# A GNN kernel on one core: a GpSimd drain behind each indirect transfer of the scatter and of the edge stage

## The chip, the cores and the metric

The kernel runs on one core of a Trainium2 chip. The metric is the time of one execution on the device, in microseconds (us). The names of the engines in the profile are PE (TensorE, matrix products; PEld is its weight load), DVE (VectorE), ACT (ScalarE), POOL (GpSimd) and SP (SyncE, which here issues DMAs). A name with a q behind it (POOLq) is the sequencer of that engine, which issues its instructions and waits on its semaphores.

## The reference

Four graph layers run one behind the other over a graph of 6,250 nodes with 128 features and 106,250 edges (two directions of 50,000 random edges, and a loop at each node), sorted by `dst`. Behind each stands a residual addition and a layer norm.

```python
edge_index = jnp.stack([src, dst])
x = _layernorm(x + _L0_gnn_ref(...), axis=-1)   # m = h @ weight[i]; agg = segment_sum(m[src], dst); h = gru_cell(agg, h)   (3 times)
x = _layernorm(x + _L1_gnn_ref(...), axis=-1)   # hypergraph: segment sums of h[row] by col, of e_feat[col] by row, batch norm, relu
x = _layernorm(x + _L2_gnn_ref(...), axis=-1)   # attention: softmax over src of leaky_relu(s1[src] + s2[dst]), sum of mapped[dst]
# L3:
e_in = jnp.concatenate([x[src], x[dst]], axis=-1)
edge_new = relu(e_in @ We1 + be1) @ We2 + be2
agg = jax.ops.segment_sum(edge_new, dst, num_segments=x.shape[0])
x = _layernorm(x + (x + mlp(concatenate([x, agg]))), axis=-1)
```

## The kernel before, in words

**The matrix.** The layers 0 to 2 don't work on the list of edges but on a dense matrix of edge counts, `adj_t` (and its transpose `adj_s`), 16-bit floats in DRAM. It is stored in 13 groups of rows; each group is read in 13 turns of 512 KB. It is first filled with zeros by DMA. Then the counts are put in: VectorE works out, from the sorted edges, for each of 832 columns of 128 edges a cell number and a value (`cell_at`, `cell_val`), and GpSimd writes each column with one indirect transfer, 128 cells of two bytes (`scatter_cells`, L1394 to L1396).

**The order of the scatter** stands in the loop at L1411 to L1437, written out by hand. The 832 columns are cut into ten units: six slabs of 104 columns and four pieces. Before a slab GpSimd waits until VectorE has its cells (`cells_ready`), before the first ones also until the zeros are there (`zeroed`). In the middle of a unit it waits with `unit_written` (L1407 to L1409) until the transfers of the unit before have landed, and counts `slab_done` up. Ahead of the fifth slab (`n == SL // 2`) stand 8 small transfers (L1427) and 7 gathers of pairs of edges (L1431), with waits for VectorE (`ext_moved`, `pairs_ready`); the first stage of the other engines ends with what these bring. Behind the last unit but one stand three transfers for cells beyond the columns (`scatter_ext`, L1400), and behind the last unit, which is waited for, three more gathers (L1444).

**The first pass** over the matrix (L493 to L650) starts when that first stage has ended. SP loads a tile of `adj_t` per turn (L498), ScalarE casts it for the matrix products of layer 0, PE multiplies it (L567, L568) and turns it over (transposes, L575), VectorE moves what is turned out of PSUM (L623), and ScalarE stores it as `adj_s`. There are 181 turns: 12 groups of 13, then 12 turns for the rows behind them, and the last group (number 11 of 0 to 12) with 13. SP holds each group back until the scatter has passed the units that touch it:

```python
            def group_there(g):
                sp.wait_ge(S("slab_done"), sp.value_load(need[0:1, g:g + 1], min_val=1, max_val=len(UNITS)))
```

and the last group until all of them are written. After the first pass come the remaining passes of the layers 0 to 2, in which GpSimd has no work.

**The edge stage** (layer 3) does work on edges, 110 chunks of 8 tiles of 128 edges. For every tile GpSimd gathers 128 rows of 512 bytes from a table of the nodes (`edge_pool`, L887), 880 gathers in all, into a ring of four chunks (`row_ring`, `HOT` = 4). It waits ahead of each chunk for `idx_ready`, the chunk's indices that ScalarE copies into a ring of four (`indices`, L905). ScalarE does that for chunk c + 4 at the end of its own turn of chunk c, when the rows of chunk c have landed and VectorE has added them. For each tile PE multiplies one-hot matrices with the part of `dst` (L942); VectorE adds the gathered rows to it (L965 to L980), ScalarE applies the relu (L927), PE sums the edges of a block (L953) and VectorE adds the sums to `acc` (L990). All five engines go over the chunks with `edge_turns` (L869 to L877), and semaphores link them.

Of the kernel before, what the change touches and what calls it, by code (L numbers as in the profile page):

```python
# [123 lines left out]
def wait(eng, sem, value):  # L124

    if isinstance(value, int) and value <= 0:
        return
    if isinstance(sem, Count):
        eng.wait_ge(sem.sem, value + sem.base)
    else:  # L130
        eng.wait_ge(sem, value)  # L131
# [10 lines left out]
def gnn(nc, d):  # L142
    ctx = ExitStack()
    with ctx:
# [199 lines left out]
        def S(name):  # L344
            if name not in made:
                made[name] = sem(name)
            return made[name]
# [521 lines left out]
        def edge_turns(eng, body):  # L869

            for c in range(PEELED):
                body(c, c % HOT, 0, c)
            with eng.Fori(0, EDGE_LOOPS) as i:
                for h in range(HOT):
                    c = PEELED + h
                    body(HOT * i + c, c % HOT, i + c // HOT, None)
            for c in range(PEELED + HOT * EDGE_LOOPS, CHUNKS):  # L877
                body(c, c % HOT, c // HOT, c)

        def edge_pool(pool):  # L880
            idx_ready = S("idx_ready")

            def body(c, slot, use, at):
                wait(pool, idx_ready, c + 1)
                pool.sem_inc(rows_opened, 1)
                for u in range(CH):
                    nc.gpsimd.indirect_dma_start(  # L887
                        row_ring[slot][:, u, :], None, table[0:N, :],
                        bass.IndirectOffsetOnAxis(idx_ring[:, slot * CH + u:slot * CH + u + 1], 0),
                    ).then_inc(half_landed[2 * slot + u // 4], 16)  # L890
            edge_turns(pool, body)

        def edge_sp(sp):
# [422 lines left out]
        def _(pool):  # L1316
# [77 lines left out]
            def scatter_cells(out, cells, name, c):  # L1394
                nc.gpsimd.indirect_dma_start(out, bass.IndirectOffsetOnAxis(cells[:, c:c + 1], 0), cell_val[:, c:c + 1],  # L1395
                                             None).then_inc(S(name), 16)  # L1396

            def scatter_ext(out, j, name):
                for k in range(EXT_BLOCKS):
                    nc.gpsimd.indirect_dma_start(out, bass.IndirectOffsetOnAxis(ext_i[:, j + k:j + k + 1], 0),  # L1400
                                                 ext_val[:, k:k + 1], None).then_inc(S(name), 16)

            def zeroed(at):
                pool.wait_ge(S("zeroed"), pool.value_load(need[P - 1:P, at:at + 1], min_val=1, max_val=len(ZEROED)))
                pool.sem_inc(rows_opened, 1)

            def unit_written(n):  # L1407
                pool.wait_ge(S(f"at_written{n % 2}"), 16 * sum(UNITS[n % 2:n + 1:2]))
                pool.sem_inc(S("slab_done"), 1)  # L1409

            def unit_from(n):  # L1411
                return n * SLW if n < KEPT else KEPT * SLW + sum(PIECES[0:SCATTER_ORDER[n - KEPT]])

            for n in range(len(UNITS)):
                if n < KEPT:
                    pool.wait_ge(S("cells_ready"), n + 1)
                else:
                    pool.wait_ge(S("relaid"), 16 * (5 + 2 * len(PIECES)))
                if n < 2:
                    zeroed(GROUPS + n)  # L1420
                if n == 2:
                    pool.wait_ge(S("zeroed"), len(ZEROED))
                if n == SL // 2:
                    pool.wait_ge(S("cells_ready"), SL + 1)
                    pool.wait_ge(S("ext_moved"), 48)
                    for t in range(SL):
                        nc.gpsimd.indirect_dma_start(ext_node, bass.IndirectOffsetOnAxis(ext_i[:, 24 + t:25 + t], 0),  # L1427
                                                     ext_i[:, 24 + SL + t:25 + SL + t], None).then_inc(S("ext_stored"), 16)
                    pool.wait_ge(S("pairs_ready"), 1)
                    for g in range(TG):  # L1430
                        nc.gpsimd.indirect_dma_start(pair_rows[:, g, :], None, edges.rearrange("(t e) a -> t (e a)", e=P),  # L1431
                                                     bass.IndirectOffsetOnAxis(pair_idx[:, g:g + 1], 0)
                                                     ).then_inc(S("pairs_in"), 16)
                for c in range(UNITS[n]):
                    if n and c == min(SC, UNITS[n] // 2):
                        unit_written(n - 1)
                    scatter_cells(adj_t, cell_at, f"at_written{n % 2}", unit_from(n) + c)  # L1437
                if n == len(UNITS) - 2:
                    pool.wait_ge(S("cells_ready"), SL + 2)
                    scatter_ext(adj_t, 16, "at_ext")  # L1440
            unit_written(len(UNITS) - 1)

            for k in range(EXT_BLOCKS):
                nc.gpsimd.indirect_dma_start(ext_w[:, k:k + 1], None, hyper_row[0:N, :],  # L1444
                                             bass.IndirectOffsetOnAxis(ext_i[:, k:k + 1], 0)).then_inc(S("ext_stored"), 16)
            edge_pool(pool)


# [1194 lines left out]
```

## Time and profile before

| | before |
|---|---|
| median of 3 runs | 6,140.44 us |
| lowest, highest run | 6,117.9 and 6,144.16 us |
| profiled execution | 6,150.24 us |
| its span in the trace | 6,148.5 us |
| its mean granted clock of TensorE | 0.79 of full speed |

The profile is taken from one execution. Its span runs from the first to the last instruction, 1.7 us less than that execution's own time. A page sums it up: busy time by engine, the costliest groups of instructions (source line, engine, operation, what is written from what, the count, the busy time in us and the mean duration in ns, and then the idle time of the engine ahead of them with what ended it). "Issue" as such a cause is time in which the engine waited for no other engine that the profile shows. Stretches can be cut out of the trace, with each engine's busy time and number of instructions (x) in them.

### The profile page before, as it was taken

What the parts mean: (1) busy time and instruction counts of PE and PEld (TensorE: products, weight loads), DVE (VectorE), ACT (ScalarE), POOL (GpSimd) and SP (SyncE); (2) the same over time, 40 slices, a digit from 0 to 9 for tenths busy, and PEclk for the clock granted to TensorE, in tenths of its full rate; (3) what the DMA queues carried; (4) which work ended last, traced back from release to release, by engine and by line L of the source; (5) the groups of instructions that cost most, each with busy time, mean ns of one, the idle gap of its engine ahead of it and who ended that gap; (6) DMA issues with size and microseconds to landing.
All of it is one profiled execution on the core that took longest, in us unless ns stands there. A gap on an engine that the chain in (4) does not pass through costs nothing. (4 is left out here: it accounts for less than half of the span.)

```text
span 6148.5 us, 81008 instructions
## 1 busy us (share of the span) xinstructions
PE 4033.3 (66%) x23848; PEld 3300.6 (54%) x23849; DVE 3243.5 (53%) x7745; ACT 2296.2 (37%) x3162; POOL 1771.6 (29%) x1769
## 2 busy tenths in 40 slices
PE   5432482111599889899699897899973444444446
PEld 3211251000477677787588685899973443344335
DVE  6321375000499888787766446688862333333334
ACT  0000011000366555555455554788852222222223
POOL 4677303777200000000000000000025555655562
PEclk7655696555799999999899897999986666666667
DMA  9600000000599468388188782244432222222221
GB/s 363 248 1 0 0 3 27 14 14 21 191 368 368 161 231 283 111 287 283 56 290 285 210 286 82 90 149 148 145 107 74 76 78 73 81 79 74 74 81 49
DMA packets 316927, 854.94 MB, mean 139 GB/s; under 512 B 84546, under 2 KB 108800, under 8 KB 316666
## 3 DMA queue, kind: packets, MB, share of 16 engines
q1 hardware_dynamic: 204092, 616.07, 29.7%
q10 hardware_dynamic: 57120, 177.22, 7.7%
q0 software_dynamic: 55456, 58.46, 3.8%
q8 instruction: 130, 2.13, 0.1%
q14 instruction: 129, 1.06, 0.0%
HBM read 666.57 MB, written 185.01 MB: 139 GB/s over the span
## 5 line engine op out<-in xcount | busy, mean ns | idle before, releaser
L887 POOL DMA_INDIRECT big<-table,idx_ring x880 | 875.2, 995 | 3592.9 <-ACT idx_ring L905 3331.9
L1395 POOL DMA_INDIRECT adj_t<-cell_val,cell_at x832 | 861.1, 1035 | 366.5 <-issue 352.2
L744 PE MATMUL ps<-tiles_r,stage_r 128*128 128x512 f32 x2028 | 807.4, 398 | 33.4 <-ACT tiles_r L702 27.6
L623 DVE TENSOR_SCALAR_CACHE_REDUCE big<-ps 128x512 f16<-128x512 f16 (+2 forms) x724 | 430.1, 652 | 602.3 <-remote 493.8
L990 DVE TENSOR_TENSOR acc<-ps,acc 128x128 f32 x880 | 255.4, 290 | 734.0 <-remote 484.9
L927 ACT ACTIVATE stage<-stage 128x512 f32<-128x512 f32 x220 | 135.7, 630 | 1102.3 <-DVE stage L980 915.2
L1757 PE MATMUL ps<-big,ident_h 128*128 128x104 bf16 (+1 forms) x2880 | 364.6, 265 | 272.7 <-issue 270.8
L953 PE MATMUL ps<-big,stage 128*128 x1760 | 330.1, 356 | 280.1 <-issue 132.4
L751 PE MATMUL ps<-stage,big 128*128 128x130 f32 x4046 | 464.0, 277 | 17.6 <-DVE big L839 15.4
L751 PEld LDWEIGHTS ps<-stage,big 128*128 128x128 f32 x4046 | 459.7, 193 | 18.3 <-issue 14.5
L953 PEld LDWEIGHTS ps<-big,stage 128*128 128x128 f32 x1760 | 297.9, 259 | 307.0 <-issue 306.8
L702 ACT CAST tiles_r<-onehot 128x1024 fp32r<-128x1024 f16 x338 | 354.8, 1050 | 288.1 <-PE ps L746 144.8
L744 PEld LDWEIGHTS ps<-tiles_r,stage_r 128*128 128x128 f32 x2028 | 387.1, 191 | 128.3 <-issue 25.5
L1757 PEld LDWEIGHTS ps<-big,ident_h 128*128 128x128 bf16 x2880 | 234.3, 107 | 404.7 <-issue 341.1
L2152 DVE TENSOR_TENSOR big<-stage 128x1248 bf16<-128x1248 f32 x192 | 272.2, 1455 | 329.6 <-remote 231.4
L746 PE MATMUL ps<-tiles_r,lower_r 128*128 128x512 f32 x1016 | 402.1, 396 | 0.0
L676 ACT ACTIVATE big<-big,cols,stage 128x512 f32 (+1 forms) x508 | 371.5, 802 | 80.5 <-PE ps L751 68.9
L746 PE MATMUL ps<-tiles_r,lower_late 128*128 128x512 f32 x1012 | 400.9, 396 | 0.0
L942 PE MATMUL ps<-rows,stage 128*128 128x128 f32 x864 | 173.0, 333 | 290.2 <-issue 286.5
L942 PE MATMUL ps<-onehot,stage 128*128 128x128 f32 x896 | 182.5, 333 | 258.4 <-issue 244.2
L523 ACT CAST tiles_r<-onehot 128x2048 fp32r<-128x2048 f16 (+2 forms) x91 | 162.6, 1789 | 451.7 <-DVE big L623 269.1
L942 PEld LDWEIGHTS ps<-rows,stage 128*128 128x128 f32 x864 | 150.8, 244 | 316.3 <-issue 312.4
(427 smaller groups left out, 7908.6 us busy)
## 6 DMA issues: line engine op xcount, KB each, us to landing
onehot<-adj_t SPq DMA_DIRECT2D x332, 512.0 KB
big<-adj_t SPq DMA_DIRECT2D x332, 512.0 KB
onehot<-adj_s SPq DMA_DIRECT2D x170, 512.0 KB
adj_t<-rows ACTq DMA_DIRECT2D x13, 6656.0 KB
adj_s<-big ACTq DMA_DIRECT2D x157, 512.0 KB
stage<-local_rows SPq DMA_DIRECT2D x110, 512.0 KB
big<-adj_s SPq DMA_DIRECT2D x84, 512.0 KB
x_fm<-adj_s SPq DMA_DIRECT2D x84, 512.0 KB
```

Of the source, the lines that this page charges most:

```text
L623: last = nc.vector.tensor_scalar(turned[turn % RING][:, j, of, :].rearrange("p m c -> p (m c)"), flips[turn % 2][:, j, of, :].rearrange("p ...
L676: nc.scalar.activation(tile32[s][:, m * GW:(m + 1) * GW], r_rows[:, bass.ds(g * GW, GW)], ACT.Relu, bias=col(MINUS_ONE), scale=stage_nm[:, ...
L702: nc.scalar.copy(tile_r[s][:, 0:TW // 2], raw_tile(p, s)[:, 0:TW // 2]).then_inc(S("cast_act"), 1)
L744: nc.tensor.matmul(psum_fm(p, n)[:, 0:cut], upper_rows[:, k, :], tile[:, 0:cut], start=k == 0, stop=False, skip_group_check=True)
L746: last = nc.tensor.matmul(psum_fm(p, n)[:, 0:cut], lower_of(p)[:, k, :], tile[:, 0:cut], start=False, stop=k == NBP - 1, skip_group_check= ...
L751: last = nc.tensor.matmul(psum_nm(p, n, j), tile[:, j * P:(j + 1) * P], stage_nm[:, k, 0:AW], start=k == 0, stop=k == NBP - 1, skip_group_ ...
L887: nc.gpsimd.indirect_dma_start(row_ring[slot][:, u, :], None, table[0:N, :], bass.IndirectOffsetOnAxis(idx_ring[:, slot * CH + u:slot * CH ...
L942: nc.tensor.matmul(psum_sum(h, u, P), ring_e[:, h * CH + u, :], hot_ring[slot][:, u, :], start=True, stop=True, skip_group_check=True).the ...
L953: last = nc.tensor.matmul(ps[:, 4 + 2 * h + g, (u % 4) * P:(u % 4 + 1) * P], ring_ohT[:, h * CH + u, :], q_nm[:, bass.ds(blk[u] * P, P)], ...
L1395: nc.gpsimd.indirect_dma_start(out, bass.IndirectOffsetOnAxis(cells[:, c:c + 1], 0), cell_val[:, c:c + 1], None).then_inc(S(name), 16)
L1757: return nc.tensor.matmul(ps[:, bank, of], stationary, moving, start=False, stop=True, skip_group_check=True)
L2152: nc.vector.tensor_tensor(eq[done % 4], own.unsqueeze(1).to_broadcast([P, SHIFTS, SLW]), bass.AP(behind.tensor, behind.offset, [behind.ap[ ...
```

## The change

It puts one instruction, `nc.gpsimd.drain()`, behind each of the 880 gathers of the edge stage and behind each of the 832 scatters. It has no semaphore; on GpSimd's instruction stream it stands between a transfer and the next. None stands behind the other indirect transfers (L1400, L1427, L1431, L1444). No instruction is removed or put in another order on any engine.

```diff
@@ -888,6 +888,7 @@
                         row_ring[slot][:, u, :], None, table[0:N, :],
                         bass.IndirectOffsetOnAxis(idx_ring[:, slot * CH + u:slot * CH + u + 1], 0),
                     ).then_inc(half_landed[2 * slot + u // 4], 16)
+                    nc.gpsimd.drain()
             edge_turns(pool, body)
 
         def edge_sp(sp):
@@ -1435,6 +1436,7 @@
                     if n and c == min(SC, UNITS[n] // 2):
                         unit_written(n - 1)
                     scatter_cells(adj_t, cell_at, f"at_written{n % 2}", unit_from(n) + c)
+                    nc.gpsimd.drain()
                 if n == len(UNITS) - 2:
                     pool.wait_ge(S("cells_ready"), SL + 2)
                     scatter_ext(adj_t, 16, "at_ext")
```

## Rows read from the trace of the kernel before

**Rows 1.** The page, busy us, share of the span and instructions of each engine

```profile
PE 4033.3 (66%) x23848; PEld 3300.6 (54%) x23849; DVE 3243.5 (53%) x7745; ACT 2296.2 (37%) x3162; POOL 1771.6 (29%) x1769
```

**Rows 2.** The page, groups of instructions: GpSimd's two kinds of transfer

```profile
L887 POOL DMA_INDIRECT big<-table,idx_ring x880 | 875.2, 995 | 3592.9 <-ACT idx_ring L905 3331.9
L1395 POOL DMA_INDIRECT adj_t<-cell_val,cell_at x832 | 861.1, 1035 | 366.5 <-issue 352.2
```

**Rows 3.** Stretches of the span: start and end, length, busy us and instructions by engine

```profile
core 0: us, PE busy (x) PEld busy (x) DVE busy (x) ACT busy (x) POOL busy (x), PEclk, DMA share, GB/s
...
902.00:1034.00 132.00, 47.61 (x198) 29.50 (x196) 91.16 (x227) 38.22 (x107) 26.80 (x27) 0.66 0.05 13
1034.00:1585.00 551.00, 80.59 (x239) 38.11 (x240) 20.47 (x65) 20.68 (x11) 421.63 (x410) 0.51 0.07 18
1585.00:2080.00 495.00, 461.12 (x3820) 366.44 (x3819) 427.62 (x1414) 302.07 (x170) 0.00 (x0) 0.97 0.92 338
...
2180.00:4569.00 2389.00, 2207.91 (x12323) 1884.57 (x12323) 1714.95 (x4014) 1456.87 (x2092) 0.00 (x0) 0.95 0.59 194
4569.00:6080.00 1511.00, 680.42 (x3529) 602.70 (x3530) 526.90 (x1211) 389.40 (x547) 875.17 (x880) 0.65 0.25 76
```

**Rows 4.** Waits of GpSimd: what waited for what, us in total, times, longest

```profile
POOL big L887 <- ACT idx_ring L905: 3331.9, 37, 2984.9
POOL adj_t L1395 <- issue: 352.2, 831, 67.3
POOL big L887 <- issue: 261.0, 843, 1.7
POOL ext_node L1427 <- DVEq L2274: 213.0, 1, 213.0
POOL acc L1431 <- DVE pair_blk L2330: 96.9, 1, 96.9
POOL adj_t L1395 <- DVEq L2261: 14.3, 1, 14.3
```

**Rows 5.** Timeline of PE from 1,080 us: start, us, instruction, [idle before <-what ended it]

```profile
1081.87 0.27 PE L575 MATMUL ps<-ident_c,big 128*128 128x128 f16 x1 [2.53 <-issue]
1084.67 0.27 PE L575 MATMUL ps<-ident_c,big 128*128 128x128 f16 x1 [2.53 <-issue]
```

**Rows 6.** Stretches, as rows 3: a part of the first pass without GpSimd

```profile
1615.00:2078.00 463.00, 452.82 (x3792) 361.79 (x3790) 419.08 (x1393) 299.55 (x168) 0.00 (x0) 1.00 0.97 356
```

**Rows 7.** Stretches, as rows 3: three within or behind one cycle of the edge stage

```profile
5063.00:5072.00 9.00, 5.70 (x46) 5.13 (x46) 5.69 (x13) 3.51 (x5) 6.87 (x8) 1.00 0.42 130
5080.00:5090.00 10.00, 1.62 (x5) 1.15 (x4) 0.00 (x0) 0.00 (x0) 7.56 (x9) 0.50 0.20 59
5095.00:5102.00 7.00, 5.07 (x22) 4.82 (x23) 4.32 (x10) 1.50 (x4) 0.00 (x0) 0.50 0.00 0
```

**Rows 8.** Line 885, GpSimd's wait for a chunk: ns min/median/max, first and last start

```profile
L885 POOLq EVENT_SEMAPHORE  x110: 17/17/17, 4568.6 to 6041.2; - x110
```

**Rows 9.** Timeline of GpSimd, its last eight gathers

```profile
6041.97 0.95 POOL L887 DMA_INDIRECT big<-table,idx_ring  x1 [10.12 <-ACT idx_ring L905]
6043.23 0.95 POOL L887 DMA_INDIRECT big<-table,idx_ring  x1 [0.31 <-issue]
...
6051.03 1.56 POOL L887 DMA_INDIRECT big<-table,idx_ring  x1 [0.30 <-issue]
```

**Rows 10.** Timeline of GpSimd, the end of the scatter

```profile
1576.49 1.09 POOL L1395 DMA_INDIRECT adj_t<-cell_val,cell_at  x1 [0.30 <-issue]
1577.89 1.09 POOL L1395 DMA_INDIRECT adj_t<-cell_val,cell_at  x1 [0.30 <-issue]
1581.00 0.99 POOL L1444 DMA_INDIRECT ext_w<-hyper_row,ext_i  x1 [2.02 <-issue]
```

**Rows 11.** The program's end (line 144): ns min/median/max, first and last start

```profile
L144 POOLq DRAIN  x1: 14951/14951/14951, 6044.9 to 6044.9; - x1
```

**Rows 12.** Stretches, as rows 3: one us each behind the last gather

```profile
6054.00:6055.00 1.00, 1.00 (x6) 1.00 (x6) 0.68 (x3) 1.00 (x2) 0.00 (x0) 0.50 0.16 16
6055.00:6056.00 1.00, 1.00 (x7) 1.00 (x6) 0.58 (x2) 0.97 (x2) 0.00 (x0) 0.50 0.00 0
```

## The prediction

> **What bounds the kernel now.** I read the page first. Its busy shares name no engine as the bound: PE is busy for 66% of the span and POOL for 29% [rows 1]. But POOL's 1,771.6 us are almost all two lines, 832 scatters of 1,035 ns (L1395) and 880 gathers of 995 ns (L887) [rows 2], and these are the two lines that the change touches. So I cut the span into stages [rows 3]. Three kinds show. From 86 to 1,585 us POOL scatters; in the stretch from 1,034 to 1,585 us it is busy for 421.63 of 551 us while PE is busy for 80.59. From 1,585 to 4,569 us POOL does next to nothing and PE is busy for some nine tenths. From 4,569 to 6,080 us POOL gathers, and PE is busy for 680.42 of 1,511 us. Where POOL works, it is the bound; elsewhere the change can do nothing.
>
> POOL's own waits [rows 4] say how: between scatters it waits 352.2 us for "issue", 831 times, and for other engines at L1395, L1427 and L1431 for 14.3, 213.0 and 96.9 us. Between gathers it waits 261.0 us for "issue" (0.30 each) and 37 times for L905, one of them the 2,984.9 us before the edge stage, so that 36 waits of some 9.6 us (3,331.9 − 2,984.9 = 347 us) lie within it. Start to start, a gather takes 1.26 us and a scatter 1.27 to 1.40.
>
> The waits of the others show something odd, and a verdict on the change hangs on it. In the first pass, while POOL scatters, PE issues **one matmul in 2.80 us**, 0.27 us of it work and 2.53 us "issue", waiting for nobody [rows 5]. From 1,615 us, when POOL has stopped, PE runs 3,792 instructions in 463 us, where 551 us held 239 [rows 6]. The edge stage repeats it in small. A cycle there is 24 gathers, then a stand of some 10 us; the stretch from 5,063 to 5,104 us holds one. In the first 9 us PE runs 46 instructions, then 5 in 10 us at the end of the burst, then 22 in 7 us once POOL has stopped [rows 7]. POOL's 10 us of waiting is therefore time in which ScalarE's L905 catches up with work that could not be issued before. I take from this that indirect transfers in an unbroken series hold up the issue of every other engine, and that it ends some us after the series does.
>
> **The change part by part.** It adds 1,712 drains and moves nothing else. Only the time from one transfer's start to the next, called **p** here, changes. Three effects:
>
> *Scatters.* The chain from 86 us is POOL's from end to end: 832 p, plus some 30 us for the 21 other transfers (27 POOL instructions with 26.80 us busy stand at 902 to 1,034 us [rows 3], 15 of these transfers among them) and the landings waited for. Waits at L1427 and L1431 vanish if VectorE is no longer held up; if it stays held up they shrink as POOL comes later. The scatter ends at 86 + 832 p + 30. The last group of rows (13 turns) can only start then. A turn takes 495/181 = 2.7 us without the hindrance [rows 3], so 13 take 37 us, and with loads and drain-out I take 60 us. First pass ends at 176 + 832 p; now it ends at 2,080.
>
> *Gathers.* 880 p, and nothing else, where p is over the 0.75 us per gather (6 us per chunk of 8) that the other engines need unhindered: in the first 9 us of a cycle PE ran 46 of the 96 instructions that the 3 chunks of a cycle have [rows 7], so a chunk takes some 6 us. Now the stage takes 4,569.4 to 6,052.6, 1,483 us.
>
> *Sum.* (176 + 832 p − 2,080) + (880 p − 1,483) = **1,712 p − 3,387**, if the others' issue comes free. Zero lies at p = 1.98 us, against 1.26 to 1.40 now. This is how the drain can win at all: it costs POOL, but frees the rest.
>
> *What is p?* No row has a drain between two transfers, so bounds from both sides. **Lowest**: the drain waits for the engine alone, and the next transfer must be issued after it instead of ahead. From the sequencer's semaphore to POOL's start is 0.8 us (6,041.2 to 6,041.97) [rows 8, 9]. So p = 1.035 + 0.8 = 1.84 for scatters and 0.995 + 0.8 = 1.80 for gathers. **Middle**: it waits until the transfer has landed. The kernel has a place where POOL waits for a landing: behind the last scatter the next transfer starts 3.11 us after it, where its neighbours stand 1.40 apart [rows 10]. **Highest**: the one drain that the trace has behind gathers, at the program's end, began at 6,044.9 and took 14.951 us, to 6,059.9 [rows 11]. The last gather started at 6,051.03 and left the engine at 6,052.6 [rows 9]; the DMA engines are still busy for 0.16 of 6,054 to 6,055 and for 0.00 after [rows 12]. The drain ended 7.3 us after the engine had finished and 4.8 us after the last byte. If a drain behind one transfer is like it, the lowest case is out. If all 4.8 us recur behind every transfer, p = 3.1 + 4.8 = 7.9. But eight transfers stood before that drain since POOL had resumed at 6,041.97 [rows 9]; shared among them it is 0.6 us each, which would make p = 3.7.
>
> I take the middle, which is nearest to the only drain row once its tail is shared: 3.11 for scatters, and 3.4 for gathers, because the last gather had up to 3.97 us to the end of traffic (6,055 − 6,051.03), 0.6 of it from an engine time of 1.56 instead of 0.95. Then 832 × 3.11 + 880 × 3.4 − 3,387 = 2,588 + 2,992 − 3,387 = +2,193 us. Against the profiled execution's 6,150.24 that is 8,343, rounded to **8,350 us**. The median of the runs is 10 us below the profiled execution, which is less than what p leaves open. The scatter part is 2,588 + 176 − 2,080 = +684, the gather part 2,992 − 1,483 = +1,509. Its own range, p from 2.65 (a landing a little sooner than at the row) to 4.5 (the shared tail and 0.8 us of issue on top), is 7,300 to 10,500.
>
> The cover: nothing hides POOL in these two stretches, as PE has 80.59 of 551 us of work in the one. PE's turns of the first pass (181 × 2.7 = 490 us) hide beside 832 p once they are free, and every group but the last is done before POOL ends. The granted clock, 0.51 of 2.4 GHz from 1,034 to 1,585 us [rows 3], is the lower level; at 0.27 us of work in 2.8 us it costs nothing there, and in the changed kernel little, as POOL stays the bound.
>
> *A rule against the trace.* The DRAIN row shows POOL's drain outlasting the last byte by 4.8 us [rows 11, 12]. The Trainium skill ("PSUM — Partial Sum Buffer", section "Engine vs sequencer instructions") says that a drain waits until the engine's execution is entirely idle, and ("Perfetto Trace Analysis", "DMA Instruction — SWDGE (GPSIMD)") that such a transfer's record closes when the last of GpSimd's processors has written its descriptors, which is ahead of the landing. By these two the drain would not wait for the data at all, the lowest case would hold, and the sum would be the first rival's. The trace speaks against that by the one row that it has.
>
> **The rivals.**
> 1. *Faster: the drain waits for the engine alone, and the breaks free the other engines.* p = 1.84 and 1.80: scatter ends at 86 + 1,531 + 30 = 1,647, first pass at 1,707 instead of 2,080 (−373); gathers 880 × 1.80 = 1,584 instead of 1,483 (+101). Together −272, so 5,878 us. For it: the stalls that end with the bursts [rows 5 to 7], and that the short breaks of 10 us suffice in the edge stage. Against it: the drain row. Below p = 1.98 it decides. Chance 0.27.
> 2. *As 1, but the hindrance stays*, as a break of 0.8 us may be too short for it to end. Then the first pass runs behind the scatter, 1,647 + 495 = 2,142 (+62), with +101 for the gathers: 6,313 us. Chance 0.05.
> 3. *The whole tail recurs behind every transfer*: p = 7.9, 1,712 × 7.9 − 3,387 = +10,138, some 16,300 us. For it: the drain row taken as it stands. Against it: that its eight transfers may have made it. A part of the tail lies between: half gives p = 5.5 and 12,180. Chance 0.18 for p over 5.7.
> 4. *The drain does nothing*: issue stays ahead of the engine, p stays, and the time too, 6,150 us. Against it: the drain row ended after the engine and not with its issue. Chance 0.04.
>
> **How the numbers follow.** The forecast, with p between 2.2 and 5.7, has what is left, 0.46. Only case 1 is faster: 0.27. Case 4 is the same: 0.04 (±0.5%, or 31 us, is about what a measurement of this kernel can tell from no change). Slower: 0.46 + 0.05 + 0.18 = 0.69. The cases have both signs, and the likeliest one's own range is 7,300 to 10,500. The range for 8 times in 10 must take in case 1 and leave out the far tail only: from 5,840 (case 1 with 40 us to spare) to 12,500 (p = 5.7).
>
> **What would show it.** In the profile of the changed kernel: drains as POOLq rows at L891 and behind the scatter; the "issue" between POOL's transfers, 0.30 us now, would be about 2.1 us if I am right (p less 1.0), 0.8 in rival 1, 7 in rival 3. POOL's waits for L905 within the edge stage go from 347 us to nearly nothing in every case but 4. PE's first pass would be spread beside the scatter, with normal turns of under 3 us, and end some 60 us after the last scatter; the edge stage would be 880 p. The stretch from the end of the first pass to the edge stage (2,080 to 4,569 us) keeps its 2,489 us. I am wrong if p is not between 2.65 and 4.5, or if PE still issues one matmul in 2.8 us while POOL takes p of 2 or more: then the hindrance goes with the number of transfers outstanding rather than with their rate, and each us of the scatter is followed by the whole 495 us of the first pass.

## The result and the profile after

| | before | changed kernel |
|---|---|---|
| median of 3 runs | 6,140.44 us | 8,576.43 us |
| lowest, highest | 6,117.9, 6,144.16 | 8,569.17, 8,584.78 |
| span of the profiled execution | 6,148.5 us | 8,583.1 us |

The ratio is 1.3977, with a 95% interval of 1.3937 to 1.4017: the changed kernel is slower by 2,436 us. 8,350 was forecast.

The changed kernel's line numbers are one higher behind its line 890 and two higher behind its line 1438. Its page, busy times and the two groups of GpSimd, beside [rows 1, 2]:

```profile
PE 4128.1 (48%) x23848; PEld 3454.3 (40%) x23849; DVE 3249.8 (38%) x7745; ACT 2299.4 (27%) x3162; POOL 1828.2 (21%) x1769
...
L887 POOL DMA_INDIRECT big<-table,idx_ring x880 | 934.5, 1062 | 4642.5 <-ACT idx_ring L906 2530.7
L1396 POOL DMA_INDIRECT adj_t<-cell_val,cell_at x832 | 858.2, 1032 | 2011.8 <-issue 2011.8
```

The work is the same, 1,828 us instead of 1,772 on GpSimd. What grew is the idle time ahead of its transfers. The waits of GpSimd, beside [rows 4] (us in total, times, longest), have hardly any other engine left:

```profile
POOL big L887 <- ACT idx_ring L906: 2530.7, 1, 2530.7
POOL big L887 <- issue: 2111.8, 879, 4.6
POOL adj_t L1396 <- issue: 2011.8, 832, 67.6
POOL ext_node L1428 <- issue: 4.2, 8, 2.0
```

The 36 waits for ScalarE within the edge stage are gone, and so are those of 213.0 and 96.9 us for VectorE. In their place "issue" went from 352.2 to 2,011.8 us for the scatters and from 261.0 to 2,111.8 for the gathers. "Issue" hides the drain here, as the drain is an instruction of the sequencer. The rows of the four source lines (duration in ns, least, median, most; first and last start; and what the landing of a transfer took after its start) show what it is:

```profile
L887 POOL DMA_INDIRECT big<-table,idx_ring x880: 953/953/1988, 5451.7 to 8497.1; - x176
...
DMA to landing us min/median/max: 2.4/2.5/5.7
```

```profile
L891 POOLq DRAIN  x880: 2365/2807/6037, 5451.5 to 8496.8; - x176
```

```profile
L1396 POOL DMA_INDIRECT adj_t<-cell_val,cell_at x832: 969/969/8794, 86.7 to 2914.5; - x167
...
DMA to landing us min/median/max: 2.1/2.1/7.3
```

```profile
L1439 POOLq DRAIN  x832: 2075/2439/14830, 86.4 to 2914.2; - x167
```

A drain's row begins 0.2 to 0.3 us before its transfer (the first: 86.4, 86.7). Paired one by one, the drains end 2.21 us after their scatter's start (median of 832), and the landing is at 2.1. Behind the gathers it is 2.59 us, and the landing is at 2.5. **The drain ends with the landing, some 0.1 us behind it.** The timeline of GpSimd (start, us, instruction, idle before) adds the rest:

```profile
109.38 1.47 POOL L1396 DMA_INDIRECT adj_t<-cell_val,cell_at  x1 [6.28 <-issue]
117.05 1.36 POOL L1396 DMA_INDIRECT adj_t<-cell_val,cell_at  x1 [6.21 <-issue]
...
1003.60 0.97 POOL L1396 DMA_INDIRECT adj_t<-cell_val,cell_at  x1 [1.98 <-issue]
1006.52 0.97 POOL L1396 DMA_INDIRECT adj_t<-cell_val,cell_at  x1 [1.96 <-issue]
...
5999.10 0.95 POOL L887 DMA_INDIRECT big<-table,idx_ring  x1 [2.40 <-issue]
6002.44 0.95 POOL L887 DMA_INDIRECT big<-table,idx_ring  x1 [2.38 <-issue]
```

Start to start an undisturbed scatter takes 2.93 us: 2.1 to the landing and 0.8 from there to the next start. An undisturbed gather takes 3.30 us (the median; 3.34 in the rows above). While the matrix is still being zeroed (DMA share 0.99) a scatter takes 7.7 us. The stretches (columns as in rows 3) show the places:

```profile
86.00:228.00 142.00, 105.20 (x911) 77.29 (x909) 112.61 (x134) 0.00 (x0) 30.30 (x19) 0.83 0.99 392
228.00:1446.00 1218.00, 250.16 (x1999) 174.31 (x1998) 273.01 (x432) 40.66 (x113) 424.44 (x398) 0.60 0.02 6
1470.00:2915.00 1445.00, 462.66 (x3761) 368.93 (x3761) 417.74 (x1380) 297.15 (x168) 404.33 (x418) 0.66 0.32 114
2915.00:2960.00 45.00, 38.53 (x312) 30.98 (x312) 33.06 (x105) 24.64 (x13) 3.33 (x4) 0.90 0.79 301
5451.00:8500.00 3049.00, 862.66 (x3512) 769.71 (x3512) 527.74 (x1194) 391.65 (x548) 934.47 (x880) 0.53 0.13 38
```

Quiet scatters (228 to 1,446 us) come every 1,218/398 = 3.06 us, waits for units included. Those beside the first pass's loads (1,470 to 2,915) come every 1,445/418 = 3.46. The first pass runs beside the scatter, 3,761 PE instructions in it, and ends 45 us behind it.

**Where the 2,435 us of span went.** The first pass's last VectorE reading of PSUM starts at 2,959.2 instead of 2,077.2 us: +882. From there to the first gather it is 2,492.5 instead of 2,492.2 us: 0. From the first gather to the last one's start it is 3,045.4 instead of 1,481.6 us: +1,564. From there to the end it is 86.0 instead of 97.5 us: −11. The sum is +2,435.

### The profile page after: what moved, and what is told of

Read it like the earlier page. It is cut to its first block and busy times, and to the rows that moved or that the text cites. A ratio compares the mean times of both kernels' runs of the same rounds, so it can differ in the third digit from the quotient of the medians.

```text
span 8583.1 us, 82720 instructions
## 1 busy us (share of the span) xinstructions
PE 4128.1 (48%) x23848; PEld 3454.3 (40%) x23849; DVE 3249.8 (38%) x7745; ACT 2299.4 (27%) x3162; POOL 1828.2 (21%) x1769
## 5 line engine op out<-in xcount | busy, mean ns | idle before, releaser
L887 POOL DMA_INDIRECT big<-table,idx_ring x880 | 934.5, 1062 | 4642.5 <-ACT idx_ring L906 2530.7
L1396 POOL DMA_INDIRECT adj_t<-cell_val,cell_at x832 | 858.2, 1032 | 2011.8 <-issue 2011.8
L981 DVE TENSOR_TENSOR stage<-ps,big 128x512 f32<-128x512 f32 x220 | 152.2, 692 | 2399.0 <-DMA big<-table,idx_ring 2399.0
L943 PE MATMUL ps<-onehot,stage 128*128 128x128 f32 x896 | 232.2, 441 | 1007.6 <-ACT stage L928 1007.6
L943 PE MATMUL ps<-rows,stage 128*128 128x128 f32 x864 | 224.0, 441 | 961.9 <-ACT stage L928 961.9
L943 PEld LDWEIGHTS ps<-onehot,stage 128*128 128x128 f32 x896 | 199.5, 328 | 1038.9 <-ACT stage L928 959.2
L943 PEld LDWEIGHTS ps<-rows,stage 128*128 128x128 f32 x864 | 192.4, 328 | 992.1 <-ACT stage L928 916.6
L954 PE MATMUL ps<-big,stage 128*128 x1760 | 408.5, 426 | 221.6 <-DVE onehot L966 111.4
L954 PEld LDWEIGHTS ps<-big,stage 128*128 128x128 f32 x1760 | 379.6, 328 | 253.3 <-issue 253.3
L575 PE MATMUL ps<-ident_c,big 128*128 128x128 f16 x1344 | 94.1, 224 | 734.6 <-DMA big<-adj_t 734.2
```

The costliest lines, as they stand in the source:

```text
L887: nc.gpsimd.indirect_dma_start(row_ring[slot][:, u, :], None, table[0:N, :], bass.IndirectOffsetOnAxis(idx_ring[:, slot * CH + u:slot * CH ...
L943: nc.tensor.matmul(psum_sum(h, u, P), ring_e[:, h * CH + u, :], hot_ring[slot][:, u, :], start=True, stop=True, skip_group_check=True).the ...
L954: last = nc.tensor.matmul(ps[:, 4 + 2 * h + g, (u % 4) * P:(u % 4 + 1) * P], ring_ohT[:, h * CH + u, :], q_nm[:, bass.ds(blk[u] * P, P)], ...
```

## The experiments

**The two stages, one at a time.** `e1_scatter_drain` has only the second, `e2_edge_drain` only the first of these:

```diff
@@ e2: edge_pool, behind each gather
+                    nc.gpsimd.drain()
@@ e1: the loop of the scatter, behind each scatter_cells
+                    nc.gpsimd.drain()
```

> The drains behind the 832 scatters alone. My theory: the two stages are added one to the other, and each costs what it cost in the changed kernel, where the first pass ended at 2,959.8 instead of 2,077.9 us (+882) and the gathers took 3,046 instead of 1,483 us. So 6,140 + 882 = 7,022 us here, with the edge stage at its old 1,483 us. The rival, that one part leans on the other (a queue or ring of GpSimd that the drains keep empty serves both), has the edge stage off its 1,483 us by over 20 us.

> The drains behind the 880 gathers alone. My theory: the gathers take 3,046 instead of 1,483 us (+1,563) and the tail is 11 us shorter, so 6,140 + 1,552 = 7,692 us; the drains' median is 2.8 us as in the changed kernel, and the first pass ends at its old 2,078 us.

Measured: 7,021 and 7,673 us, beside 6,146 for the kernel before. The two additions, 875 and 1,527, make 2,402 of the 2,436 us. The stages add up within 34 us. In `e1_scatter_drain` the gathers run from 5,448.8 to 6,917.9 us, 1,469 instead of 1,482; that is 13 us, under the 20 that the rival asked for.

**A wait for the landing in place of the drain.**

```diff
@@ edge_pool
+                    wait(pool, half_landed[2 * slot + u // 4], 64 * use + 16 * (u % 4 + 1))
+                    pool.sem_inc(rows_opened, 1)
@@ the loop of the scatter
+                    pool.wait_ge(S(f"at_written{n % 2}"), 16 * (sum(UNITS[n % 2:n:2]) + c + 1))
```

> In place of each drain GpSimd waits on the transfer's own semaphore. My theory, that the drain costs what it costs because it waits until the transfer has landed, and then 0.8 us for the next one's issue: the same start-to-start times, 2.93 us undisturbed in the scatter and 3.33 in the gathers, and 8,576 us within 1%. The rival, that the drain has a price of its own on top of or instead of the landing: start-to-start times over 0.2 us off these, which is over 340 us in the sum; shorter if the drain adds something behind the landing (the 4.8 us behind the last byte at the program's end before point that way).

Measured: 8,162 us, 415 less than the changed kernel. Timeline of GpSimd in `e3_landing_wait`, and its row of line 887:

```profile
1006.13 0.97 POOL L1397 DMA_INDIRECT adj_t<-cell_val,cell_at  x1 [1.43 <-DMA adj_t<-cell_val,cell_at]
1008.54 0.97 POOL L1397 DMA_INDIRECT adj_t<-cell_val,cell_at  x1 [1.44 <-DMA adj_t<-cell_val,cell_at]
...
6003.79 0.95 POOL L887 DMA_INDIRECT big<-table,idx_ring  x1 [2.25 <-DMA big<-table,idx_ring]
```

```profile
L887 POOL DMA_INDIRECT big<-table,idx_ring x880: 950/950/2003, 5042.1 to 8079.6; - x176
```

The gathers are as in the changed kernel: 3,037.5 us from first to last start against 3,045.4. There the edit puts a count-up (`pool.sem_inc`) behind the wait, and this is an instruction of the sequencer (17 ns, L892), as the drain is, with the next transfer behind it. The scatters come every 2.40 us instead of 2.93. Their landing is still 2.1 us after the start, but the wait, against a constant, has no row of its own and the next transfer starts 0.3 us after the landing instead of 0.8. So most of the drain's price is the landing, and a further 0.5 us is that nothing may be issued ahead of it. The scatters' whole series, 2,423.8 instead of 2,827.8 us, makes 404 of the 415 us. The theory holds in its first half; the claim that waiting in any form costs the same falls. (That it is the sequencer's own instruction which makes the 0.5 us is read from these two forms, of which one stands in the scatter and the other among the gathers; no run has both in one place.)

The run shows one thing more. It has no drain at all and ran on a chip where the kernel before takes 6,146 us, and PE is not held up beside its scatter, which has 168 transfers in this stretch (columns as in rows 3):

```profile
1100.00:1600.00 500.00, 214.26 (x1778) 172.05 (x1778) 199.66 (x654) 139.98 (x78) 162.35 (x168) 0.71 0.43 155
```

So it is not the drain as an instruction that frees the others.

**A drain behind every eighth transfer.**

```diff
@@ edge_pool
+                    if u == CH - 1:
+                        nc.gpsimd.drain()
@@ the loop of the scatter
+                    if c % 8 == 7:
+                        nc.gpsimd.drain()
```

> A drain behind every eighth transfer of both stages instead of every one. The rate within a burst of eight stays as before (1.27 us), the mean is (7 x 1.27 + 2.93)/8 = 1.48 us for scatters and (7 x 1.26 + 3.33)/8 = 1.52 for gathers. My theory, that the other engines are held up only by an unbroken series of some ten transfers or more, so that a short stand in every eight frees them: 832 x 1.48 + 880 x 1.52 - 3,387 = -818, so 5,320 us, or up to 5,400 with the landings that other traffic delays. The rival, that they are held up wherever transfers follow at 1.27 us: the hindrance stays, the first pass still runs behind the scatter, and the time is between 6,050 and 6,400 us.

Measured: 5,542 us beside 6,146, so **faster than both kernels**. Stretches of `e4_drain_8`, and then a piece of its GpSimd timeline in the edge stage:

```profile
228.00:830.00 602.00, 279.85 (x2096) 195.60 (x2094) 286.57 (x459) 42.29 (x113) 390.84 (x376) 0.69 0.06 17
830.00:1500.00 670.00, 506.74 (x3589) 385.58 (x3587) 383.31 (x1283) 283.82 (x159) 402.45 (x416) 0.87 0.71 235
4057.00:5456.00 1399.00, 785.88 (x3512) 703.08 (x3512) 527.15 (x1194) 391.19 (x548) 854.81 (x880) 0.63 0.27 83
```

```profile
4806.12 0.95 POOL L887 DMA_INDIRECT big<-table,idx_ring  x1 [0.30 <-issue]
4807.38 0.95 POOL L887 DMA_INDIRECT big<-table,idx_ring  x1 [0.30 <-issue]
4811.05 0.95 POOL L887 DMA_INDIRECT big<-table,idx_ring  x1 [2.71 <-issue]
```

While GpSimd scatters at a mean of 670/416 = 1.61 us, PE runs 3,589 instructions in 670 us, where [rows 3] have 239 in 551 us with transfers unbroken. Eight gathers at 1.26 us and one stand of 2.7 us leave the other engines enough: the edge stage takes 1,399 us instead of 1,483, bound by GpSimd, and its long waits for ScalarE are gone. A drain behind eight costs only 0.4 us more than one behind one (from start to start, medians: 3.73 against 3.30 for gathers, 3.34 against 2.93 for scatters).

The theory's direction held, but its number did not: 5,320 to 5,400 us were expected, and 5,542 is 142 us above that. Over the whole scatter a transfer came every 1.70 us instead of 1.48, since the stands of the scatter are 4.06 us long in the mean (up to 8.8), and a gather every 1.59 instead of 1.52. 832 × 0.22 + 880 × 0.07 makes some 240 us, about what the expectation missed. The same kernel timed in three rounds, on another chip:

> The kernel of e4_drain_8, timed. Where the kernel before takes 6,140 us: 5,545 us, ratio 0.903. Where it takes 4,970 us: the drains are pure cost and GpSimd is the bound either way, 5,500 to 5,550 us, ratio 1.11 to 1.12. The rival for that second case, that a part of the hold-up was still in e4_drain_8, gives less than 5,450 us.

Measured: 5,540.4 us beside 6,119.6, ratio 0.9045, with an interval of 0.9007 to 0.9083. One further run of it:

> The kernel of e4_drain_8 once more. It took 5,542 us where the kernel before took 6,146. Where the kernel before takes some 4,970 us there is no hold-up to take away, the drains are pure cost, and GpSimd is the bound either way: 5,500 to 5,550 us, so slower than before by 11% instead of faster by 10%. The rival, that a part of the hold-up was still in e4_drain_8, gives less than 5,450 us there.

Measured: 5,550 us beside 6,133, as in the other two. The case of a kernel before of 4,970 us did not occur in either run, so what is expected for it stays untested.

**Is it the unbroken series, or what piles up?** The next three ran as one set, on one chip.

```diff
@@ e5_lag4_scatter: the units' two semaphores become four, one transfer each in flight
+                    at = unit_from_order(n) + c
+                    if at >= 4:
+                        pool.wait_ge(S(f"at_written{at % 4}"), 16 * (at // 4))
-                    scatter_cells(adj_t, cell_at, f"at_written{n % 2}", unit_from(n) + c)
+                    scatter_cells(adj_t, cell_at, f"at_written{at % 4}", unit_from(n) + c)
@@ e6_drain_16: edge_pool
+                    if u == CH - 1 and slot % 2:
+                        nc.gpsimd.drain()
@@ e6_drain_16: the loop of the scatter
+                    if c % 16 == 15:
+                        nc.gpsimd.drain()
@@ e8_memset_scatter, behind each scatter
+                    spot = unit_from(n) + c
+                    nc.gpsimd.memset(idle_tile[32 * (spot % 4):32 * (spot % 4) + 32, spot // 4:spot // 4 + 1], 0.0)
```

> Scatter alone, edge stage as before, no drains: each scatter waits for the landing of the fourth before it, so that at most four are under way. A landing takes 2.1 us and four starts take 5.1, so the wait is nearly always over already and the rate stays at 1.27 us. Theory A, that the unbroken rate holds up the other engines: nothing changes, 6,140 us within 60, first pass ending at about 2,080 us. Theory B, that it is a number of transfers or of issued instructions piling up, which any wait for a landing bounds: the hindrance goes at full rate, the first pass ends at 176 + 832 x 1.27 = 1,233 us or up to 160 later, as with a drain at every eighth, and the time is 5,300 to 5,460 us.

> A drain behind every sixteenth transfer (every second chunk in the edge stage). Mean start-to-start times by the rates seen: (15 x 1.27 + 3.2)/16 = 1.39 for scatters, (15 x 1.26 + 3.7)/16 = 1.41 for gathers, 0.1 to 0.18 less than with a drain at every eighth. If the other engines' hold-up begins some ten transfers into a series and ends soon after it, they lose a third of the time and POOL stays the bound: edge stage about 1,260 instead of 1,397 us, first pass some 100 us sooner, 5,300 to 5,400 us. The rival, that the hold-up from the tenth transfer on is enough to make the others the bound again: POOL waits for idx_ring again in the edge stage, and the time is 5,542 us or over.

> Scatter alone, edge stage as before, no drains: behind each scatter a memset of one column of 32 partitions into a tile of its own, which nothing waits for and which waits for nothing. It slows the rate to some 1.45 to 1.6 us with no wait for a landing. Theory A, the rate: the hindrance goes or shrinks, the first pass ends near 1,500 to 1,650 us, the time is 5,600 to 5,750 us. Theory B, that a wait for the landing is what frees the others: the first pass still runs behind the scatter and ends at or after 2,080 us, and the time is 6,130 to 6,350 us.

Measured: 5,068, 5,320 and 4,976 us. But the kernel before, run beside them on the same chip, took **4,977 us**, not 6,146. The hold-up, PE's issue held back beside an unbroken series as in [rows 5], does not occur on that chip at all. The edge stage of `e5_lag4_scatter`, which is the kernel before's own, shows it: no stand of GpSimd for ScalarE within the stage, and 1,125 us for what took 1,482 (line 887 with what its engine waited for, then a stretch of the first pass):

```profile
L887 POOL DMA_INDIRECT big<-table,idx_ring x880: 948/955/1834, 3857.7 to 4982.3; - x176
...
  ACT idx_ring L905: 2530.2, 1
```

```profile
830.00:1328.00 498.00, 363.76 (x2966) 289.30 (x2964) 329.73 (x1100) 232.74 (x134) 334.43 (x346) 0.87 0.74 261
```

With 346 scatters at a mean of 1.44 us, PE runs 2,966 instructions in 498 us. So this set can't tell the theories apart, and that 5,320 us lies in the range of `e6_drain_16`'s theory says nothing for it. It leaves three facts: the four-in-flight wait costs 91 us there, the memset costs nothing (0.1 us, in a gap of 0.3), and drains at every sixteenth cost 343 us. In `e8_memset_scatter` the rate also stayed at 1.27 us, so that it would have been no test of a slower rate on any chip.

**The changed kernel on such a chip.**

> The changed kernel as it is. In the second set of runs the kernel before took 4,977 us instead of 6,146, on another chip, and the traces there show no held-up issue. My theory says that the drains make GpSimd the bound everywhere, so that the hold-up has no part in the changed kernel's time: 8,576 us within 1% beside a kernel before of 6,146 us, and 8,450 to 8,600 us beside one of 4,977 us, a ratio of 1.72. The rival, that the second chip is faster in general (GpSimd, DMA), gives 8,576 x 4,977/6,146 = 6,945 us there.

Measured: **8,568 us beside 4,966**, a ratio of 1.725. The rival with a faster chip falls. The drained kernel is bound by GpSimd and the landings, which are the same on both (a drain behind a gather takes 2.80 us in the median here, 2.81 there). From the first pass's last reading of PSUM to the first gather, where GpSimd has no work, it is 2,488.5 us here and 2,492.5 there. So as far as these rows show, the chips differ in the hold-up alone. The forecast's own sum gives the difference too: with the rate of the kernel before and the hold-up gone, 1,712 × 1.27 − 3,387 = −1,213 us, 4,937 for a measured 4,977.

**Four in flight where the hold-up is.** The first repeat ran on the chip without hold-up:

> The kernel of e5_lag4_scatter once more, since the set that held it ran on a chip where the kernel before took 4,977 us and had no hold-up to take away; there the wait alone cost 91 us. Where the kernel before takes 6,146 us: theory A (the unbroken rate holds up the others) 6,140 us within 100; theory B (a wait for a landing is enough, at full rate) 5,300 to 5,560 us. Beside a kernel before of 4,977 us it says nothing new and should give 5,068 us within 0.5%.

Measured: 5,073 beside 4,966. The third ran on a chip with it:

> The kernel of e5_lag4_scatter a third time, for a chip where the kernel before takes some 6,140 us: theory A (the unbroken rate holds up the others) 6,140 us within 100; theory B (a wait for a landing is enough, at full rate) 5,300 to 5,560 us. Beside a kernel before of 4,970 us it repeats 5,070 us.

Measured: 6,140 us beside 6,133. Its stretches, against [rows 3]:

```profile
1034.00:1585.00 551.00, 76.00 (x222) 34.56 (x222) 22.80 (x72) 17.08 (x9) 416.80 (x406) 0.51 0.07 17
4569.00:6040.00 1471.00, 665.69 (x3441) 587.33 (x3442) 512.67 (x1171) 383.06 (x538) 875.02 (x880) 0.65 0.27 79
```

406 scatters at 1.27 to 1.40 us as before, and 222 PE instructions in 551 us: held up as before, though at most four transfers are under way. A bound on what is in flight does not help; a short stand after eight does, where the transfers before it came at the same 1.27 us. Theory B falls. Theory A stands as far as this: an unbroken series at this rate holds up the others, on the chips that show it. Whether the stand itself or the lower mean rate frees them no kernel was able to test, since the one meant for that did not slow the rate. But the trace of the kernel before speaks for the rate. PE's matrix products of one line (L1757) run beside the scatter in two stretches:

```profile
440.00:468.00 28.00, 18.01 (x96) 8.50 (x97) 8.75 (x6) 0.00 (x0) 22.02 (x20) 0.50 0.02 0
546.00:690.00 144.00, 14.94 (x51) 5.35 (x51) 4.42 (x3) 0.00 (x0) 109.53 (x112) 0.50 0.02 0
```

In the first, every third scatter takes some 1.55 us instead of 0.97, so that their starts stand 1.27, 1.27 and some 1.85 us apart, with never more than 0.31 us of idle time between them: PE runs 96 products in 28 us. In the second nearly all stand 1.27 us apart, and PE runs 51 in 144 us. There is no stand in either. This is a reading of one trace, in which other things differ too, and not a test.

The chips in one view (single runs but for the first and the last; us):

| set | kernel before | kernels beside it |
|---|---|---|
| the result | 6,140 | changed 8,576 |
| e1 to e4 | 6,146 | scatter drained 7,021, edge drained 7,673, landing waits 8,162, every eighth 5,542 |
| e5, e6, e8 | 4,977 | four in flight 5,068, every sixteenth 5,320, memset 4,976 |
| e7, e9 | 4,966 | changed 8,568, four in flight 5,073 |
| e10, e11 | 6,133 | every eighth 5,550, four in flight 6,140 |
| e12 | 6,120 | every eighth 5,540 |

## Why the prediction was right, step by step

*POOL is the bound in both stages, and the change is 1,712 p − 3,387.* It holds. With the measured means, 2,827.8/832 = 3.40 us (the 15 small transfers of the fifth slab included) and 3,045.4/879 = 3.46, it gives 832 × 3.40 + 880 × 3.46 − 3,387 = +2,487 against +2,435. The 52 us too many are for the most part the 30 us for the other transfers, which that mean already has in it, the 60 us behind the last scatter, which took 45, and the tail, which is 11 us shorter.

*p from the landing, 3.11 and 3.4.* The choice between engine alone, landing and whole tail was right, and the rows of the drains show the landing as its end. The 0.8 us of issue that the lowest case added is there too, behind the landing (0.72 and 0.69 us behind the drain's end). The two values were right in sum more than in kind, and the 3.4 was partly luck: it took the end of all DMA traffic behind the last gather for the next start, with no issue time. Measured, an undisturbed gather lands at 2.5 us and the next starts 0.8 later, so that a landing taken too late and an issue left out made up for each other. The undisturbed scatter takes 2.93, less than the row of 3.11, which also held the wait and the count-up of a unit. The mean of 3.40 is higher, because landings wait behind other traffic: one start per 7.7 us while the zeros are written, one per 3.46 beside the first pass. So the scatter part was under-sized, +684 forecast and +882 measured, and the term that was off is the p of 3.11. The gather part was +1,509 forecast and +1,564 measured.

*The rule on drains.* By the trace the drain ends with the landing of the data, which is 2.1 and 2.5 us after a start, while the engine's own record is 0.97 and 0.95 us. By the Trainium skill's sentence that a drain waits for the engine to be idle ("PSUM — Partial Sum Buffer", "Engine vs sequencer instructions"), read together with "Perfetto Trace Analysis", "DMA Instruction — SWDGE (GPSIMD)", it would have ended with that record. The measurement decides, so for an indirect transfer of GpSimd the data's landing belongs to what the drain waits for.

*Rival 3, the whole tail behind every transfer.* It did not occur. The end drain of the changed kernel takes 53 ns, and a drain behind eight costs 0.4 us more than one behind one:

```profile
L144 POOLq DRAIN  x1: 53/53/53, 8500.6 to 8500.6; - x1
```

My sharing of the tail among eight transfers (0.6 us each) was wrong as well: it would have made a drain behind eight 4.2 us dearer than one behind one. The tail is also there without the hold-up: in `e5_lag4_scatter` the end drain ends 8.3 us after the last gather's start (4,968.2 + 22.4 − 4,982.3), in the kernel before 8.8. The runs show two things of it. It grows with the number of transfers since the drain before. Behind one, eight and sixteen gathers (the last from `e6_drain_16`) the drain ends 0.40, 0.69 and 1.01 us after the last packet of GpSimd's queue, in the median, and behind the 880 of the kernel before it is 5.0 us. And it is not the landing of something still under way. In `e3_landing_wait`, where GpSimd has itself waited for every landing, the last one until 8,083.1 us, the end drain still takes 7.3 us:

```profile
L144 POOLq DRAIN  x1: 7267/7267/7267, 8083.2 to 8083.2; - x1
```

So "the drain ends with the landing" holds where drains stand close to each other. What the drain does in the rest stays open. The long tail is seen only at the program's end where the edge stage has no drains, and it costs nothing there: the program runs on for 88 us more behind it.

*The others' issue comes free.* Right: the first pass runs beside the scatter and ends 45 us behind it, and GpSimd's waits for L905 are gone. That the series holds up "every other engine" was more than the rows showed. It is seen on PE, on SyncE and in part on VectorE, and not on ScalarE (the rows stand in the last section). But its share in this result is small, since a kernel that waits 2.93 us or more per transfer is bound by that anyway. `e7_after_again` shows this best: without any hold-up to remove, the changed kernel takes the same 8,568 us. The hold-up costs the kernel before 6,140 − 4,970 = 1,170 us, where it occurs.

*The clock.* The granted clock fell to 0.53 in the edge stage, and PE is busy there for 863 of 3,049 us, where it was 680 of 1,511. The products are slower and it costs nothing, as said.

## What to carry to other kernels

A drain on GpSimd behind an indirect transfer is a wait for its landing: behind every one of them it turns a stream of one per 1.27 us into one per 3 to 3.5 us, and more where other traffic delays the landings. Where the kernel must wait for a landing, let the wait ride on the next transfer (0.3 us instead of 0.8 behind the landing). Where a stand is wanted, one behind every eighth transfer costs some 0.3 us per transfer instead of 1.7 to 2.0 (2.93 and 3.30 less 1.27 and 1.26). Before believing in a stall of "issue" that no semaphore explains, run the kernel on more than one chip: the drain at every eighth is 9.6% faster than the kernel before where the hold-up is, and on a chip without it, where GpSimd's own 5,540 us would stand against 4,970, it should lose some 11%. That was not run; the nearest that was, a drain at every sixteenth, lost 7% there (5,320 against 4,977 us).

## What the hardware showed that was not expected

The same kernel before took 6,100 to 6,157 us on some chips and 4,966 and 4,977 us on two others. The traces lay the difference to one thing: on the first, some ten transfers into an unbroken series of GpSimd's indirect transfers at 1.27 us, other engines get to issue an instruction only every 0.7 us or a multiple of it; on the others they don't. PE's products stand 2.80 us apart in [rows 5], and about 2.8, 2.1 or 1.4 us apart from 5,077 to 5,094 us, where the series began at 5,061. The clearest rows are those of one register instruction, at the end of a chunk's turn in the edge stage (duration in ns, least, median, most). These are from the kernel before, of SyncE, VectorE and ScalarE:

```profile
L873 SPq FUSED_REGOPS  x25: 16/698/727, 4577.8 to 5902.0; - x25
L873 DVEq FUSED_REGOPS  x25: 18/98/1395, 4656.9 to 5965.8; - x25
L873 ACTq FUSED_REGOPS  x25: 68/68/73, 4653.9 to 5962.9; - x25
```

And this is SyncE's on a chip without the hold-up, in `e5_lag4_scatter`, whose edge stage is the same:

```profile
L873 SPq FUSED_REGOPS  x25: 50/50/50, 3866.1 to 4847.0; - x25
```

It does not depend on how many transfers are in flight (four at most: 6,140 against 6,133 us), and a stand of 2 to 3 us after every eighth removes it, or a wait for each landing. Why chips differ in it, no run here tells; each chip without it has one set of runs, so that the chip and the moment aren't told apart either. And a wait against a constant, ahead of an indirect transfer, let it start 0.3 us after the landing, where behind a drain, or a wait with an instruction of the sequencer behind it, it took 0.7 to 0.8 us.
